# A state-space layer between two gated feed-forward blocks: prologue and first half step in a written-out order

## The chip, the cores and the metric

The kernel runs on one core of a Trainium2 chip. The time is that of the whole program on the device, in microseconds (us), as the median of several runs. Profiles show one execution; its span leaves out a little of the time at the start and end.

## The reference

Input x is [2, 2048, 256] in float32. Three residual parts follow each other:

```python
x = x + 0.5 * ffn(layernorm(x), w_gate, w_up, w_down)
x = x + ssm(layernorm(x), in_proj, conv, x_proj, dt_proj, A_log, D, C_proj, out_proj)
x = x + 0.5 * ffn(layernorm(x), w_gate, w_up, w_down)
# ffn: (silu(x @ wg.T) * (x @ wu.T)) @ wd.T, integer weights times 1/127, hidden width 768
# ssm: x_in, z = split(x @ in_proj.T), width 512 each
#      xc = causal convolution of x_in, 4 taps;  dt, B = split(xc @ x_proj.T)
#      delta = clip(softplus(dt @ dt_proj.T + dt_b), 0.001, 0.1);  a = exp(delta * A)
#      h[t] = a[t] * h[t-1] + (a[t] - 1) / A * B[t];  y = h @ C_proj.T + xc * D
#      out = (y * silu(z)) @ out_proj.T
```

## The kernel before

The 2048 rows of each sequence go in four tiles of 512. The program is a chain of half steps h = -1 to 8 that alternate between the two sequences. In half step h, part **A** is the first feed-forward of one sequence's tile, **B** the state-space layer of the other sequence's tile, **C** the second feed-forward of the tile whose B was one half step earlier. `Bnext` is the layer norm ahead of the next B. Half step -1 has only A, half step 0 has B and A, the last has only C.

Every engine has its program written out, and semaphores tie them. No scheduler moves anything. On TensorE a table gives the order of steps: `gate0` to `gate5` and `up0` to `up5` (a 128 x 512 chunk of the hidden width), `down00` to `down11` (a quarter of the product back to tokens), `ix` and `iz` (chunks of the input projection for x and z), `xp0` and `xp1` (dt and B), `cp0` to `cp3` (the product with C), `out00` to `out11`, and `turn0`, `turn1` (normalized rows turned on TensorE). Products go through four PSUM banks `q` in turn; a bank is free again when the one operation that reads it (ScalarE or VectorE) has run, and the function `plan` counts which one that is. Each float32 operand is taken apart in a high and a low half of 16 bits: ScalarE writes the high one (`xh`, `hh`, `xch`), VectorE or GpSimd the low one (`xl`, `hl`, `xcl`).

The prologue stands ahead of and in half step -1. Weights arrive as 32-bit integers or floats, ScalarE casts them (L487), TensorE turns 128 x 128 blocks into a bank (a "fill", L1257), ScalarE copies the bank to the weight tile (L503 to L526). VectorE reduces the integer weights to their largest size (L1091, L1114), counts those over 256, and the count becomes a flag on which TensorE and VectorE branch (`further_parts`, L1311; here it is zero and the branch is taken past). VectorE computes scales: `hidden_scales` (L936 to L942), `row_scales` (L947 to L953), `conv_bound` and `conv_scale` (L1006 to L1028, with one product on TensorE between them, L1451), `x_proj_scale` (L1040 to L1044), and the constants of A by a series on single columns (`decay_rate`, `decay_series`, `decay_finish`, L959 to L984). In the old order these last three stand in the first half step between the softplus input (L842) and delta (L847).

A fill group is issued as a whole (`early`, `up`, `down`, `in`, `delta`, `late`), and half step 0 uses the same function `half(g)` as all later ones on each engine. On VectorE: `stats` L742, `variance` L750 to L760, `normalize` L773, `norm_lo` L782, `hidden` L803, `residual` L814, the convolution taps L828, `halo` L836, `series` L860, `scan` L885, `skip_y` L899. On ScalarE: `norm_hi` L532, `gate` L550, `hidden_high` L558, `conv_begin` L566, `conv_in` L574, `input_in` L615. On GpSimd: `root` L407, the cast of w_down L413, `hidden_low` L421, `conv_low` L428, `gate_y` L436.

## Time and profile before

| | |
|---|---|
| median of 3 runs | 540.81 us (538.62 to 544.32) |
| the profiled execution | 548.71 us, span 546.8 us |
| TensorE busy | 507.3 us (93%) |
| VectorE busy | 416.7 us (76%) |
| ScalarE busy | 281.1 us (51%) |
| GpSimd busy | 227.0 us (42%) |
| mean granted clock of TensorE | 0.968 |

Times of a profile are counted from the span's start. The granted clock is a share of 2.4 GHz. In the rows, PE is TensorE, DVE VectorE, ACT ScalarE, POOL GpSimd; buffer numbers are left out of names, so `xpre` is the loaded rows of either sequence. An arrow in brackets names what ended the idle time ahead of an instruction.

### The profile page before, as it was taken

Reading aid. Unit: us, or ns where it says so; the run is one execution under the profiler, and the core shown is the slowest. Engines: PE = TensorE matmul, PEld = TensorE weight load, DVE = VectorE, ACT = ScalarE, POOL = GpSimd, SP = SyncE. Lnnn points to the kernel's source line nnn. Section 1 sums busy time; section 2 is a strip of 40 time slices with the busy share of each in tenths; the row PEclk is TensorE's granted clock in tenths of the full one; section 3 lists DMA queues with packets and bytes.
Section 4 is the critical chain, followed back from the end, with each engine's and each line's share of the span. In section 5 each row is a group of like instructions: output and inputs, shape, how many; then the busy total and the mean of one; then the engine's idle time right before and its main releaser. Section 6 shows DMA issues by size and latency. Waiting matters only on the chain.

```text
span 546.8 us, 7716 instructions
## 1 busy us (share of the span) xinstructions
PE 507.3 (93%) x2657; PEld 296.1 (54%) x2657; DVE 416.7 (76%) x865; ACT 281.1 (51%) x472; POOL 227.0 (42%) x192
## 2 busy tenths in 40 slices
PE   4869877999999999999999999999999999998696
PEld 4346423844566465745485456646484557545444
DVE  5786678699678977798769977897869876887332
ACT  5473655076624774187606672377508761674032
POOL 2230053428271637246451828154633736073213
PEclk9887997999999999999999999999999999999869
DMA  8401000000220020101120032003020021000001
GB/s 290 119 0 41 2 0 0 2 2 0 41 80 1 2 41 32 47 1 22 30 69 0 2 41 78 1 2 40 20 59 2 10 33 40 1 1 20 19 2 40
DMA packets 27240, 16.84 MB, mean 31 GB/s; under 512 B 15264, under 2 KB 26528, under 8 KB 27184
## 3 DMA queue, kind: packets, MB, share of 16 engines
q1 hardware_dynamic: 26368, 15.26, 11.1%
q10 hardware_dynamic: 816, 0.79, 0.5%
q8 instruction: 40, 0.66, 0.5%
q14 instruction: 16, 0.13, 0.1%
HBM read 8.71 MB, written 4.19 MB: 24 GB/s over the span
## 4 chain that ended last, share of the span: by engine, by line
PE 73%; DVE 12%; DMA 5%; ACT 3%; issue 3%; SPq 2%; POOL 2%; POOLq 0%; DVEq 0%; ACTq 0%
PE q L1346 49%; PE dp L1346 19%; DMA xt<-xs 4%; DVE xn L773 3%; PE tp L1257 3%; SPq L379 2%; DVE xs L790 2%; DVE h L803 1%; DMA hh<-in_L_ffn_w_gate_dram 1%; POOL xcl L428 1%; PE q L1257 1%; ACT xc L566 0%; DVE rmx L947 0%; DVE ser L860 0%; DVE x L814 0%
## 5 line engine op out<-in xcount | busy, mean ns | idle before, releaser
L421 POOL TENSOR_TENSOR hl<-h,hh 128x512 f16<-128x512 f32 x96 | 121.1, 1274 | 107.2 <-ACT hh L558 106.9
L803 DVE SCALAR_TENSOR_TENSOR h<-sg,hsm,q 128x512 f32<-128x512 f32 x96 | 70.7, 742 | 39.3 <-PE q L1346 26.2
L828 DVE SCALAR_TENSOR_TENSOR xc<-xi,cw,xc 128x512 f32<-128x512 f32 x96 | 84.1, 890 | 3.2 <-ACT xi L574 2.6
L532 ACT ACTIVATE xh<-tp 128x512 f16<-128x512 f32 x36 | 19.5, 595 | 113.8 <-PE tp L1257 113.8
L550 ACT ACTIVATE sg<-q 128x512 f32<-128x512 f32 x96 | 56.6, 591 | 40.8 <-PE q L1346 40.8
L558 ACT ACTIVATE hh<-h 128x512 f16<-128x512 f32 x96 | 60.3, 629 | 27.4 <-DVE h L803 27.1
L428 POOL TENSOR_TENSOR xcl<-xc,xch 128x512 f16<-128x512 f32 x32 | 41.1, 1296 | 50.4 <-ACT xch L581 50.4
L1346 PE MATMUL dp<-wo,yu 128*128 128x256 f32 x256 | 60.2, 388 | 1.5 <-POOL yu L436 1.5
L1346 PE MATMUL dp<-wd,hh 128*128 128x256 bf16 x384 | 53.9, 277 | 0.9 <-ACT hh L558 0.9
L1346 PE MATMUL dp<-wd,hl 128*128 128x256 bf16 x384 | 53.7, 277 | 0.8 <-POOL hl L421 0.8
L1346 PEld LDWEIGHTS dp<-wo,yu 128*128 128x128 f32 x256 | 48.4, 195 | 9.5 <-POOL yu L436 2.7
L1346 PEld LDWEIGHTS dp<-wd,hh 128*128 128x128 f16 x384 | 38.0, 99 | 13.2 <-issue 5.5
L1346 PE MATMUL q<-xh,wu 128*128 128x512 f16 x120 | 37.9, 399 | 5.9 <-ACT bm L615 4.3
L436 POOL TENSOR_TENSOR yu<-yu,sz 128x512 f32<-128x512 f32 x32 | 39.6, 1273 | 8.6 <-DVE yu L899 8.6
L1346 PEld LDWEIGHTS dp<-wd,hl 128*128 128x128 f16 x384 | 38.2, 99 | 6.0 <-issue 1.1
L566 ACT ACTIVATE xc<-q,cb,rw 128x512 f32<-128x512 f32 x32 | 25.0, 780 | 31.3 <-PE q L1346 31.3
L1346 PE MATMUL q<-xh,wg 128*128 128x512 f16 x120 | 37.9, 399 | 2.6 <-DVE xl L782 2.0
L1346 PE MATMUL q<-xh,wih 128*128 128x512 f16 x128 | 38.3, 379 | 1.4 <-ACT xh L532 1.2
L1346 PE MATMUL q<-xt,wg 128*128 128x512 f16 x144 | 37.0, 379 | 2.4 <-DMA xt<-xs 2.4
L1346 PE MATMUL q<-xh,wil 128*128 128x512 f16 x128 | 38.1, 379 | 0.0
L1346 PE MATMUL q<-xl,wih 128*128 128x512 f16 x128 | 38.1, 379 | 0.0
L1346 PE MATMUL q<-xl,wg 128*128 128x512 f16 x120 | 37.7, 396 | 0.0
(182 smaller groups left out, 851.0 us busy)
## 6 DMA issues: line engine op xcount, KB each, us to landing
xpre<-in_L_attn_x_dram SPq DMA_DIRECT2D x8, 512.0 KB, 4.5
out_dram<-x SPq DMA_DIRECT2D x16, 256.0 KB, 2.1
xc<-in_L_attn_in_proj_w_dram SPq DMA_DIRECT2D x1, 1024.0 KB, 11.1
hl<-in_L_ffn_w_up_dram ACTq DMA_DIRECT2D x3, 256.0 KB, 6.5
hh<-in_L_ffn_w_gate_dram SPq DMA_DIRECT2D x3, 256.0 KB, 7.1
hh<-in_L_ffn_w_down_dram SPq DMA_DIRECT2D x1, 768.0 KB, 8.5
yu<-n_L_attn_out_proj_w_dram SPq DMA_DIRECT2D x1, 512.0 KB, 4.0
yu<-in_L_attn_x_proj_w_dram SPq DMA_DIRECT2D x1, 256.0 KB, 11.4
```

The lines of the kernel that those rows point to most:

```text
L421: pool.tensor_tensor(HL[g.f][:, c, :], H[:, j, :], HH[g.f][:, c, :], ALU.subtract)\
L428: pool.tensor_tensor(XCL[:, m, :], XC[g.b][:, m, :], XCH[:, m, :], ALU.subtract)\
L436: pool.tensor_tensor(YU[g.b][:, m, :], YU[g.b][:, m, :], SZ[g.b][:, m, :], ALU.mult)\
L532: act.activation(XH[g.f][:, kc, :], tp[kc][:, :], ACT.Copy, scale=XS).then_inc(t_hi[kc], 1)
L550: act.activation(SG[:, (first + c) % 2, :], q[bank][:, :], ACT.Silu, scale=QUANT / XS)\
L558: act.activation(HH[g.f][:, c, :], H[:, (first + c) % 3, :], ACT.Copy).then_inc(hh_ready, 1)
L566: act.activation(XC[g.b][:, m, :], q[bank][:, :], ACT.Identity, bias=CB[:, m:m + 1], scale=RW3[:, m:m + 1]).then_inc(xc_begun, 1)
L773: ins = dve.tensor_scalar(XN[:, b, :], src[:, b, :], MN[k][:, b:b + 1], RS[k][:, b:b + 1], ALU.subtract, ALU.mult)
L803: dve.scalar_tensor_tensor(out=H[:, first % 3, :], in0=SG[:, first % 2, :], scalar=HSM[:, c:c + 1], in1=q[bank][:, :], op0=ALU.mult, op1=A ...
L828: dve.scalar_tensor_tensor(out=XC[s][:, m, :], in0=XI[s][:, m, k:k + TILE], scalar=CW[:, m, k:k + 1], in1=XC[s][:, m, :], op0=ALU.mult, op ...
L1257: return pe.transpose(dst, src, IDN[:, :] if ident is None else ident)
L1346: ins = pe.matmul(out, w, a, start=(at == 0), stop=(at == len(terms) - 1))
```

## The change

The orders of the prologue and of half step 0 are written out one step at a time on TensorE (a table `FIRST`), ScalarE, VectorE and GpSimd. Fill groups become single fills, so that they stand between chunks of the products. Half steps 1 to 6 keep the function `half`; half steps 7 and 8 are written out too, in the order that they had. No operation is added or removed and no tile changes; the DMA queues keep their order.

```diff
+FIRST = (("fill", "g0", -1), ("fill", "u0", -1), ("fill", "g1", -1), ("fill", "u1", -1), ("count0", "", -1),
+         ("fill", "g2", -1), ("fill", "u2", -1), ("turn0", "A", -1), ("turn1", "A", -1), ("flag0", "", -1),
+         ("more0", "", -1), ("gate0", "A", -1), ("gate1", "A", -1), ("up0", "A", -1), ("gate2", "A", -1),
...
 def tensor_order(h):
-
-
-
-    if h == -1:
...
-    return [(what, part, h) for what, part in ORDER
-            if has("A" if part == "Bnext" else part, h) and (what, part, h) not in done]
...
-    for what, part, h in (step for at in range(-1, LAST + 1) for step in tensor_order(at)):
+    middle = [step for h in range(1, LAST - 1) for step in tensor_order(h)]
+    for what, part, h in (*FIRST, *middle, *FINAL):
...
+            last = "w_dve" if part[:-1] in ("i", "x", "t") else "w_act"
+            count[last] += 1
+            reader[take("ring", part, h)] = (last, count[last])
...
-            hidden_low(Half(-1), "A")
-            root(Half(-1), "Bnext")
-            half(Half(0))
-            for h in range(1, LAST + 1):
+            before, start, late, last = Half(-1), Half(0), Half(LAST - 1), Half(LAST)
+            pool.wait_ge(negh_ready, 1)
+            root(before, "A")
+            root(start, "A")
+            hidden_low(before, "A", (0,))
+            cast_down()
+            hidden_low(before, "A", (1, 2, 3, 4, 5))
+            root(before, "Bnext")
+            conv_low(start, (0, 1, 2, 3))
+            hidden_low(start, "A", (0, 1, 2, 3, 4, 5))
+            gate_y(start, (0, 1, 2, 3))
+            root(start, "Bnext")
...
+            cast("g", 0)
+            cast("u", 0)
+            fill("g0")
+            cast("g", 1)
+            cast("u", 1)
+            fill("u0")
+            cast("g", 2)
+            fill("g1")
+            fill("u1")
+            cast("u", 2)
+            fill("g2")
+            norm_hi(before, "A", (0,))
+            fill("u2")
+            norm_hi(before, "A", (1,))
...
+            norm_hi(start, "A", (0,))
+            scale_row(0)
+            scale_row(1)
+            gate(before, "A", (4,))
+            scale_row(2)
+            norm_hi(start, "A", (1,))
+            hidden_high(before, "A", (2,))
+            scale_row(3)
+            scale_row(4)
+            gate(before, "A", (5,))
+            fill("d0")
+            fill("d1")
+            scale_row(5)
+            scale_row(6)
+            fill("d2")
+            scale_row(7)
+            fill("i0")
+            copy_rank()
+            hidden_high(before, "A", (3,))
+            fill("i2")
+            hidden_high(before, "A", (4, 5))
+            fill("i1")
+            scale_x(0)
+            scale_x(1)
+            fill("i3")
...
-            first, second = Half(-1), Half(0)
-            stats(first, "A", range(NB))
-            variance(first, "A")
-            for j in range(HC // 2):
-                if j == 1:
-                    normalize(first, "A")
-                for nat, load, rows in ((NGI, ld_g, WMX[:, 0:HC]), (NUI, ld_u, WMX[:, HC:2 * HC])):
-                    dve.wait_ge(load[j], 16)
-                    ins = dve.tensor_reduce(rows[:, 2 * j:2 * j + 2], nat[:, 2 * j:2 * j + 2, :], AX.X, ALU.max,
...
+            weight_rows("g", 0)
+            weight_rows("u", 0)
+            weight_rows("g", 1)
+            weight_rows("u", 1)
+            stats(before, "A", (0, 1, 2, 3))
+            weight_rows("g", 2)
+            variance(before, "A")
+            weight_rows("u", 2)
+            stats(start, "A", (0,))
+            over(0)
+            stats(start, "A", (1,))
+            normalize(before, "A", (0, 1, 2, 3))
+            stats(start, "A", (2, 3))
+            hidden_scales()
+            weight_flag(0)
+            norm_lo(before, "A", (0, 1))
+            flags[0] = flag_value(0)
+            variance(start, "A")
+            further_parts(0)
+            weight_rows("d", 0)
+            normalize(start, "A", (0, 1))
+            hidden(before, "A", (0,))
+            normalize(start, "A", (2, 3))
+            hidden(before, "A", (1,))
...
+            variance(before, "Bnext")
+            hidden(start, "A", (0,))
+            normalize(before, "Bnext", (0, 1, 2, 3))
+            decay_rate()
+            x_proj_low(0)
+            norm_lo(before, "Bnext", (0, 1))
+            decay_series()
+            hidden(start, "A", (1,))
+            conv(start, 0, (2, 1, 0))
+            conv(start, 1, (2, 1, 0))
+            conv(start, 2, (2,))
+            x_proj_low(1)
+            conv(start, 2, (1, 0))
+            conv(start, 3, (2, 1, 0))
+            hidden(start, "A", (2,))
+            decay_finish()
+            delta_in(start)
+            stats(Half(1), "A", (0, 1))
+            hidden(start, "A", (3,))
+            delta(start)
+            series(start, (0, 1, 2, 3))
+            decay_out(start)
+            input_out(start)
+            scan(start)
+            halo(start)
+            hidden(start, "A", (4, 5))
+            skip_y(start, (0, 1, 2))
+            residual(start, "A", 0)
+            skip_y(start, (3,))
+            stats(start, "Bnext", (0, 1))
+            residual(start, "A", 1)
+            stats(start, "Bnext", (2, 3))
+            variance(start, "Bnext")
...
                 if B:
-                    if g.h == 0:
-                        decay_rate()
-                        decay_series()
-                        decay_finish()
                     delta(g)
...
+            for step in FIRST:
+                do(*step)
+            for h in range(1, LAST - 1):
+                for step in tensor_order(h):
+                    do(*step)
+            for step in FINAL:
+                do(*step)
```

VectorE, start of the program, before. `wmx` holds the largest integer weights (`hh` and `hl` are the buffers in which gate and up weights arrive), `over` the count behind the flag, `xn` the normalized rows of the first sequence:

```order
L742 BN_STATS st_A<-xpre 128x6 x4
...
L760 TENSOR_TENSOR ve_A<-vo_A,vi_A 128x4
L1091 TENSOR_REDUCE wmx<-hh 128x2
L1091 TENSOR_REDUCE wmx<-hl 128x2
L773 TENSOR_SCALAR xn<-xpre,mn_A,rs_A 128x256 x4
L1091 TENSOR_REDUCE wmx<-hh 128x2
...
L919 TENSOR_SCALAR over<-wmx 128x12
...
L782 SCALAR_TENSOR_TENSOR xl<-tp,xh 128x512 x2
```

and now, where `hsc` belongs to the hidden scales:

```order
L1050 TENSOR_REDUCE wmx<-hh 128x2
L1050 TENSOR_REDUCE wmx<-hl 128x2
...
L869 BN_STATS st_A<-xpre 128x6 x4
L1050 TENSOR_REDUCE wmx<-hh 128x2
...
L887 TENSOR_TENSOR ve_A<-vo_A,vi_A 128x4
L1050 TENSOR_REDUCE wmx<-hl 128x2
L869 BN_STATS st_A<-xpre 128x6
L1063 TENSOR_SCALAR over<-wmx 128x12
...
L900 TENSOR_SCALAR xn<-xpre,mn_A,rs_A 128x256 x4
L869 BN_STATS st_A<-xpre 128x6 x2
L1080 TENSOR_TENSOR hsc<-wmx 128x6
...
L909 SCALAR_TENSOR_TENSOR xl<-tp,xh 128x512 x2
```

Two reductions stood between the variance and the normalized rows; now four reductions stand ahead of the statistics, and statistics of the second sequence, the count and the hidden scales stand among normalized rows and low half.

ScalarE, end of half step -1, before. `hh` is the high half of the hidden product, `xc` here the rows of the input projection's weights that are scaled, `wd` and `wih` the weights of down and of the input projection, `da` the copy of the rank weights:

```order
L558 ACTIVATE hh<-h 128x512
...
L695 ACTIVATE xc<-xc,rsc 128x256 x4
L558 ACTIVATE hh<-h 128x512
L508 ACTIVATE wd<-q,hsi 128x256
L509 ACTIVATE wd<-q,hsi 128x256
...
L498 ACTIVATE da<-tp 16x128
L512 ACTIVATE wih<-q 128x512 x4
```

and now:

```order
L558 ACTIVATE xc<-xc,rsc 128x256 x2
L529 ACTIVATE wd<-q,hsi 128x256
L530 ACTIVATE wd<-q,hsi 128x256
L558 ACTIVATE xc<-xc,rsc 128x256
L533 ACTIVATE wih<-q 128x512
L545 ACTIVATE da<-tp 16x128
L590 ACTIVATE hh<-h 128x512
L533 ACTIVATE wih<-q 128x512
L590 ACTIVATE hh<-h 128x512 x2
L533 ACTIVATE wih<-q 128x512
```

The last hidden copies moved from ahead of the weights of down to between the weights of the input projection.

VectorE, half step 0, before. `xc` is now the convolution's output (12 taps), `sp` the softplus input, `er` to `ia` the constants of A, `dl` delta, `bb` the scan's input, `hs` its output:

```order
L828 SCALAR_TENSOR_TENSOR xc<-xi,cw,xc 128x512 x12
L842 TENSOR_SCALAR sp<-q,dtb 128x512
L959 TENSOR_SCALAR er<-al 128x1
...
L971 TENSOR_SCALAR ey<-ey,er 128x1 x6
...
L984 TENSOR_TENSOR ia<-ia,xri 128x1
L847 TENSOR_SCALAR dl<-sp 128x512
...
L877 SCALAR_TENSOR_TENSOR bb<-sp,bm 128x512
L803 SCALAR_TENSOR_TENSOR h<-sg,hsm,q 128x512 x2
L836 COPY xi<-xi 128x4x3
L885 SCALAR_TENSOR_TENSOR hs<-sp,carry,bb 128x512
L803 SCALAR_TENSOR_TENSOR h<-sg,hsm,q 128x512 x2
```

and now:

```order
L955 SCALAR_TENSOR_TENSOR xc<-xi,cw,xc 128x512 x7
L1145 TENSOR_TENSOR wxl<-q,wxh 128x512
L955 SCALAR_TENSOR_TENSOR xc<-xi,cw,xc 128x512 x5
L930 SCALAR_TENSOR_TENSOR h<-sg,hsm,q 128x512
L1119 TENSOR_SCALAR e<-ek 128x1
...
L1128 TENSOR_TENSOR ia<-ia,xri 128x1
L969 TENSOR_SCALAR sp<-q,dtb 128x512
L869 BN_STATS st_A<-xpre 128x6 x2
L930 SCALAR_TENSOR_TENSOR h<-sg,hsm,q 128x512
L974 TENSOR_SCALAR dl<-sp 128x512
...
L1004 SCALAR_TENSOR_TENSOR bb<-sp,bm 128x512
L1012 SCALAR_TENSOR_TENSOR hs<-sp,carry,bb 128x512
```

The constants left the place between `sp` and `dl`, and the hidden products `h` and the copy `xi` no longer stand ahead of `hs`.

## Rows read from the trace of the kernel before

**Rows 1.** The page, part 1: busy time and share of the span by engine.

```profile
PE 507.3 (93%) x2657; PEld 296.1 (54%) x2657; DVE 416.7 (76%) x865; ACT 281.1 (51%) x472; POOL 227.0 (42%) x192
```

**Rows 2.** Windows, TensorE: stretch, its us, busy us (instructions), granted clock, DMA share, GB/s.

```profile
0.00:109.39 109.39, 84.89 (x418) 0.91 0.18 57
109.39:546.80 437.41, 422.40 (x2241) 0.98 0.11 24
16.76:19.60 2.84, 2.84 (x8) 0.50 0.84 267
28.00:36.00 8.00, 3.71 (x22) 1.00 0.00 0
37.00:47.12 10.12, 9.25 (x39) 0.50 0.01 2
85.00:91.69 6.69, 6.00 (x15) 0.51 0.00 0
```

**Rows 3.** Waits of TensorE up to 109 us: who ended them, in total, times, longest.

```profile
PE q L1346 <- ACT bm L615: 4.3, 1, 4.3
...
PE tp L1451 <- DVE bb L1013: 2.2, 1, 2.2
```

**Rows 4.** Timeline of VectorE at the start: start us, busy us, instruction, [idle before].

```profile
6.06 1.41 DVE L742 BATCH_NORM_STATS2 st_A<-xpre 128x6 f32<-128x256 f32 x4 [5.13 <-DMA xpre<-in_L_attn_x_dram]
...
8.28 0.68 DVE L1091 TENSOR_REDUCE wmx<-hh 128x2 f32<-128x512 int32 x1
...
9.58 1.38 DVE L773 TENSOR_SCALAR xn<-xpre,mn_A,rs_A 128x256 f32<-128x256 f32 x4
...
14.58 1.27 DVE L782 SCALAR_TENSOR_TENSOR xl<-tp,xh 128x512 f16<-128x512 f32 x2
```

**Rows 5.** Timeline of TensorE: the first gate chunk and the first down product.

```profile
16.29 0.81 PE L1346 MATMUL q<-xh,wg 128*128 128x512 f16 x2 [2.02 <-DVE xl L782]
...
42.36 1.46 PE L1346 MATMUL dp<-wd,hh 128*128 128x256 bf16 x6
```

**Rows 6.** Timeline of ScalarE: second load of gate weights; last hidden copy, first product.

```profile
8.94 0.63 ACT L487 ACTIVATE sz<-hh 128x512 f32<-128x512 int32 x1 [0.69 <-DMA hh<-in_L_ffn_w_gate_dram]
...
35.02 0.62 ACT L558 ACTIVATE hh<-h 128x512 f16<-128x512 f32 x1
```

**Rows 7.** Tile xpre up to 30 us: issue of the second load, and time to landing.

```profile
L355 SPq DMA_DIRECT2D xpre<-in_L_attn_x_dram x1: 474/474/474, 4.1 to 4.1; - x1
...
DMA to landing us min/median/max: 5.3/7.2/9.1
```

**Rows 8.** Timeline of VectorE from 22 to 91 us.

```profile
22.57 3.06 DVE L773 TENSOR_SCALAR xn<-xpre,mn_A,rs_A 128x256 f32<-128x256 f32 x4 [0.19 <-POOL rs_A L407]
...
51.57 0.67 DVE L1001 TENSOR_TENSOR wxl<-q,wxh 128x512 f16<-128x512 f32 x1
...
63.03 10.64 DVE L828 SCALAR_TENSOR_TENSOR xc<-xi,cw,xc 128x512 f32<-128x512 f32 x12 [2.65 <-ACT xi L574]
76.29 0.75 DVE L842 TENSOR_SCALAR sp<-q,dtb 128x512 f32<-128x512 f32 x1 [2.61 <-PE q L1346]
...
81.56 0.43 DVE L847 TENSOR_SCALAR dl<-sp 128x512 f32<-128x512 f32 x1
...
86.51 0.74 DVE L803 SCALAR_TENSOR_TENSOR h<-sg,hsm,q 128x512 f32<-128x512 f32 x1
...
89.09 2.25 DVE L885 TENSOR_TENSOR_SCAN hs<-sp,carry,bb 128x512 f32<-128x512 f32 x1
```

**Rows 9.** The page, part 5: GpSimd's low halves and the convolution taps, whole run.

```profile
L421 POOL TENSOR_TENSOR hl<-h,hh 128x512 f16<-128x512 f32 x96 | 121.1, 1274 | 107.2 <-ACT hh L558 106.9
...
L828 DVE SCALAR_TENSOR_TENSOR xc<-xi,cw,xc 128x512 f32<-128x512 f32 x96 | 84.1, 890 | 3.2 <-ACT xi L574 2.6
```

**Rows 10.** Timeline of TensorE: C products of the first half step; first product of the next.

```profile
92.93 3.60 PE L1346 MATMUL q<-hs,wc 128*128 128x512 f32 x8
...
109.39 0.59 PE L1346 MATMUL q<-xh,wih 128*128 128x512 f16 x2
```

More of the change, by code:

```diff
@@ L1134, in _ @@
-            variance(first, "Bnext")
-            x_proj_low(1)
-            normalize(first, "Bnext")
-            hidden(second, "A", (0, 1))
-            norm_lo(first, "Bnext")
-            x_proj_unscale()
             def half(g):
@@ L1245, in half @@
                     stats(ahead, "C", (0, 1))
-            half(Half(0))
-            for h in range(1, LAST + 1):
-                half(Half(h))
+            before, start, late, last = Half(-1), Half(0), Half(LAST - 1), Half(LAST)
+            weight_rows("g", 0)
[6 more added lines that the diff above has]
+            weight_rows("u", 2)
@@ new lines, in _ @@
+            normalize(start, "Bnext", (2, 3))
+            stats(Half(1), "C", (0, 1))
+            for h in range(1, LAST - 1):
+                half(Half(h))
+            norm_lo(Half(6), "Bnext", (0, 1))
+            residual(Half(6), "B", 1)
+            stats(late, "C", (2, 3))
+            variance(late, "C")
+            normalize(late, "C", (0, 1))
+            conv(late, 0, (2,))
+            normalize(late, "C", (2,))
+            conv(late, 0, (1,))
+            normalize(late, "C", (3,))
@@ new lines, in _ @@
+            delta(late)
+            series(late, (0, 1, 2, 3))
+            decay_out(late)
+            input_out(late)
+            halo(late)
+            scan(late)
+            residual(late, "C", 0)
+            skip_y(late, (0, 1, 2, 3))
+            residual(late, "C", 1)
+            residual(late, "B", 0)
+            carry(late)
+            stats(last, "C", (0, 1))
+            residual(late, "B", 1)
+            stats(last, "C", (2, 3))
+            variance(last, "C")
+            normalize(last, "C", (0, 1, 2, 3))
@@ L1437, in half @@
-            def half(g):
-                run(tensor_order(g.h), g)
-            steps, first = tensor_order(-1), Half(-1)
-            products = steps.index(("gate0", "A", -1))
-            rows = steps.index(("fill", "in", -1))
-            delta_rows, tokens = steps.index(("fill", "delta", -1)), steps.index(("down00", "A", -1))
-            run(steps[:products], first)
-            count_over(0)
-            flag = flag_value(0)
-            further_parts(flag, [p for p in PARTS if p[0] != "d"])
@@ L1448, in _ @@
-            run(steps[products:rows], first)
-            pe.wait_ge(xm_ready, 1)
-            pe.matmul(tp[1][:, 0:P], XMB, IDN[:, :], start=True, stop=True).then_inc(xm_full, 1)
-            run(steps[rows:delta_rows], first)
-            count_over(1)
-            run(steps[delta_rows:tokens], first)
-            flag_down = flag_value(1)
-            further_parts(flag_down, [p for p in PARTS if p[0] == "d"])
-            run(steps[tokens:], first)
-            half(Half(0))
-            for h in range(1, LAST + 1):
-                half(Half(h))
+            flags = {}
```

461 lines of the change are left out of this document (277 added, 184 removed), and 25 rows, old and new, of tables (FINAL, FIRST).

## The prediction

> **What bounds the kernel now.** I read the page first: TensorE is busy 507.3 of 546.8 us, VectorE 416.7 [rows 1]. Then the windows [rows 2], cut where the first half step ends on TensorE (109.39 us): up to there TensorE is busy 84.89 us, after it 422.40 of 437.41 us. So the later half steps are at TensorE's floor, and 24.5 of the 39.5 idle us lie in the stretch that the change rewrites. The granted clock is at its half level (0.50, 1.2 of 2.4 GHz) there three times: 2.84, 10.12 and 6.69 us [rows 2]; busy time at half rate is half lost, (2.84 + 9.25 + 6.00) / 2 = 9.0 us. The list of waits [rows 3] says what ends TensorE's idle time: apart from the loads at the start 4.3 us for the state input that ScalarE scales and 2.2 for the bound are the longest. The last view is the timeline, for the moment at which each stage starts.
>
> The order of instructions after the first half step is the same in both programs on every engine, and TensorE hardly waits there. So what the first 109.39 us lose or gain arrives at the end one for one. The work is the same too; only its order, and the engine instruction that stands ahead of which, change. I therefore walk the new order from marker to marker with durations of the old trace. "Start to start" spacing is used, which is a little below the durations printed: 0.60 us for a weight reduction, 0.65 for a 128x512 VectorE operation, 0.55 for a ScalarE one, 0.86 for a gate or up chunk (two matmul pairs of 0.43), 1.30 for an input projection chunk, 0.48 for a weight turned through a bank, 1.31 for a quarter of the down product.
>
> **The first gate chunk: 3.4 us later.** Before, VectorE takes the statistics of the first rows at 6.06 and writes the normalized rows from 9.58; the first gate chunk starts at 16.29 [rows 4, 5]. Now four weight reductions stand ahead of the statistics. The second pair of loads lands at 8.94 [rows 6], so they end at 10.1; statistics 1.3 (11.4); a reduction (12.0); the variance 0.8 (12.8); a reduction (13.4); the root on GpSimd 1.0, hidden. Then statistics of the second sequence, whose load lands 9.1 us after its issue at 4.1, at 13.2 [rows 7]; two blocks and the count cost 0.9 (14.3); normalizing 1.3 (15.6); two more blocks 0.7; the hidden scales, now ahead of the flag, 1.4 (17.7); the flag 0.25; two low halves 1.3 (19.2). TensorE's branch on the flag waits for the second low half, as before, and came 0.5 us behind it (14.58 + 1.27 to 16.29). The first gate comes at 19.7, +3.4 us. The half-rate spell behind that wait I keep at its 2.84 us: it is idle again for some 3 us ahead of it.
>
> **From there to the variance ahead of the input projection: 5.0 us won.** Before it ends at 52.9 (the seven small operations of 0.8 us, a subtraction from 51.57 in front, [rows 8]). The gates of the first sequence now run in the order gate, gate, up, gate, up, with the turns of the next rows split in two. The four normalizing operations took 3.06 us while GpSimd's low halves ran, against 1.38 where it did not [rows 4, 8]; now they stand at 22.7 and 24.7, ahead of GpSimd's first low half at 25.3, so 1.3. The row scales end at 30.0. From there ScalarE has no gap: eight row scalings of 0.4, two gates, two norm halves, six copies for down, three of four input weights, the rank copy, and the four hidden copies, 10.5 us in all, and the last hidden copy ends at 40.5; before it was put ahead of the weights and ended at 35.6 [rows 6]. GpSimd's last three low halves, 1.2 each [rows 9], end at 42.6. So the down product, which began at 42.36 at half rate [rows 5], begins at 40.6 but cannot end its first quarter before 42.7; three more at full rate give 46.7. Residual, statistics and variance follow to 49.9, with three input-weight subtractions between them on VectorE. That is with the full clock. TensorE's idle pieces between 33 and 41 us are shorter than before (2.4 us; 4.3 between 28 and 36 us before), but not gone, and a 2.0 us gap was enough to bring the half level at 16.76 [rows 2, 5]. I take the half level here too, at 1.4 us of delay for the variance (the down quarters end 2.3 later, 0.9 of it under the subtractions). End of the variance 51.3: 1.6 us ahead of before. Bounds of this term: 0 and 4.6 (half level through all of the down product).
>
> **To the start of the convolution: 2.0 us won.** Before, four chunks and five weight fills precede the turn and the convolution starts at 63.03 [rows 8]. Now three chunks precede it; one weight subtraction, one hidden product and two fills are put off. From the variance: hidden 0.65, normalize 1.35 with the root, rate constants 1.3, a subtraction 0.65, two low halves 1.3 (they wait for ScalarE), the series of constants 1.65, hidden 0.65: 8.1 us, start at 59.4, with ScalarE's shifted copy 0.5 us ahead of it.
>
> **To delta: 2.7 us won.** Before, 12 taps of 0.88, a wait of 2.61 for the projection, then 4.6 us of one-column constants alone between the softplus input (76.29) and delta (81.56) [rows 8]. Now the taps with one subtraction take 11.3, a hidden product and the last constants (2.3) fill the wait, and behind the input come only 0.75 of statistics and 0.65 of hidden under ScalarE's exponential and logarithm (1.6). From 59.4: 70.7, 73.0, 73.7, delta at 75.3.
>
> **To the end of the scan: 2.4 us won.** Series and outputs keep their 4.9 us; two hidden products and the halo copy, 2.6 us from 86.51 to 89.09, no longer stand ahead of the scan [rows 8]. Delta to scan end was 9.7, now 7.3: 82.6 instead of 91.3. That these are put behind it costs cover: the last hidden products are now on the way to the down product. C products start right at the scan's end (before at 92.93, behind chunks at half rate), three of them take 2.6; hidden 4 and 5 end 2.2 after the scan, the last low half 2.5 later, so the down product waits 0.8 us.
>
> **To the end of the half step: 0.3 us won.** From 92.93 to 109.39 TensorE is without a gap [rows 10]: four C products, down, out, a turn, 16.5 us. The same work plus 0.8 for the low half, and 0.5 because the turn waits for a normalization that now straddles a residual: 17.8 from the scan's end, against 18.1. End at 100.4.
>
> Sum: -3.4 + 5.0 + 2.0 + 2.7 + 2.4 + 0.3 = **9.0 us won**. The profiled execution took 548.7 us, so 539.7; the three runs have a median of 540.81, 1.4% below it, and I take the same difference there: **531.8 us**. The shares saved hang on idle time, not on the level of the run.
>
> **A page's rule that speaks against it.** In this trace TensorE goes through the four banks with a reader behind each product from 109.39 on, at a mean granted clock of 0.98 [rows 2]; short waits did not pull it down there. The Trainium skill, "TensorE: Matmul & The Clock Gate", section "A second HAM failure mode: psum-queue depth-cycling", says that going through PSUM banks with small idle pieces between groups makes the clock go back and forth and loses throughput although few matmuls look slow. By that rule the finer interleaving would be slower, not faster; the trace of before does not show it in its steady part, but 37 to 47 us looks like it. What it would cost is the third case below, from rows.
>
> **The cases.** Less than 1% (5.4 us) can't be told from no change here.
> - *As walked*, 62%: 9.0 us, from 5.8 (the 4.6 bound) to 11.8 (no half level at 37 us, +1.4, and a warm start, +1.4). 529 to 535.
> - *All half levels go and the early loss is smaller*, 10%: two of the six weight reductions may slip under the wait for the second load. 10.4 + 1.4 + 1.5: 527.5.
> - *The ring eats it*, 20%: each bank is freed by one named operation, and VectorE and ScalarE run in the written order. Two places are tight: iz1 waits for the subtraction that stands behind seven taps, and the down product for hidden copies at the end of a 10.5 us ScalarE queue. Taps that GpSimd slows (890 ns in the mean [rows 9]) by another 0.2 us each cost 2.4; each ScalarE operation 0.1 late costs 2. With the half level bound of 3.2 more, 9.0 becomes 1.4: 534 to 541, same.
> - *Slower*, 8%: TensorE stays at 1.2 GHz from about 30 to 63 us of the new order. The walk has some 25 us of full-rate work there and 6 us of slack, so 19 us more: 540.8 - 10.4 + 19 = 549. It decides from where half-rate work exceeds 16 us beyond the slack, that is when the low spells there last over 30 us; before they last 10.12 [rows 2]. Against it: fewer and shorter gaps than before. A spell that reaches 25 us gives only "same".
>
> That the order doesn't take hold is excluded, since order and waits are fixed at build; that it hides is too, as TensorE waits under 4% after 109.39.
>
> **Numbers.** Predicted 531.8; range 525 to 539 (the second case, less 2.5 of spread between runs, to the middle of the third). Faster by over 1%: 0.62 x 0.95 + 0.10 + a little of the third, 0.70. Same 0.22, slower 0.08.
>
> **What would show it.** First gate chunk at 19.7 with the idle time before it ended by the second low half; last hidden copy of the first product at 40.5 and its low half at 42.6; convolution from 59.4; nothing but statistics and a hidden product between softplus input and delta; scan ending at 82.6; first product of the next half step at 100.4; no half level near 85 us; the rest as long as before (437.4). Wrong if the first gate comes at 17 or at 22, if the clock row is at 5 for most of 30 to 60 us, or if TensorE's idle time ahead of the C products stays over 3 us.

## The result, and the profile after

The changed kernel took **537.6 us** in the median of 20 runs (534.59 to 541.34), the kernel before, beside it, 544.45 us (20 runs, 538.48 to 548.79): ratio 0.9888, 95% interval 0.9867 to 0.991, so 6.1 us won by the ratio and 6.9 by the two medians. The time of the changed kernel lies in the range forecast. The gain is less than the 9.0 us of the sum, and the 531.8 us are 5.8 too low.

The profiled execution took 536.74 us (span 534.9), the one of before 548.71. The page, part 1, answers to [rows 1]: TensorE is busy 8.0 us less with the same 2657 matmuls, so it ran longer at full rate.

```profile
PE 499.3 (93%) x2657; PEld 291.1 (54%) x2657; DVE 415.5 (78%) x865; ACT 280.0 (52%) x472; POOL 226.8 (42%) x192
```

Windows of TensorE, after (stretch, its us, busy us and instructions, granted clock, DMA share, GB/s), cut at the first product of the next half step, 99.25 us. They answer to [rows 2].

```profile
0.00:99.25 99.25, 79.12 (x418) 0.95 0.20 63
99.25:534.90 435.65, 420.14 (x2241) 0.99 0.10 24
13.90:24.44 10.54, 7.98 (x28) 0.52 0.51 141
28.00:36.00 8.00, 7.37 (x42) 1.00 0.00 0
30.00:50.00 20.00, 17.00 (x112) 1.00 0.02 5
80.00:95.00 15.00, 13.25 (x77) 1.00 0.01 2
```

The first half step is 10.1 us shorter, the rest 1.8. One stretch at the half level is left in front (0.52 from 13.90 to 24.44 us), and it is longer than the 2.84 us of before, which I had kept. The two others are gone in this execution: 1.00 from 28 to 36, from 30 to 50 and from 80 to 95 us.

The waits of TensorE up to 99.25 us, after (who ended them: total us, times, longest), answer to [rows 3]:

```profile
PE q L1566 <- DVE xl L909: 2.6, 1, 2.6
PE dp L1520 <- DVE over L1063: 2.2, 1, 2.2
PE dp L1566 <- POOL hl L427: 1.9, 2, 1.0
PE q L1471 <- ACT xc L558: 1.1, 1, 1.1
```

The 4.3 and 2.2 us of [rows 3] are gone. TensorE now waits 2.2 us for the count (`over`) and 2.6 us for the low half, both ahead of the first gate chunk; behind it no wait is longer than 1.1 us.

Timeline of TensorE, after (start us, busy us, instruction, [idle before, who ended it]), against [rows 5, 10]:

```profile
19.37 1.01 PE L1566 MATMUL q<-xh,wg 128*128 128x512 f16 x2 [2.56 <-DVE xl L909]
...
40.98 0.83 PE L1566 MATMUL dp<-wd,hh 128*128 128x256 bf16 x6
...
43.33 0.28 PE L1566 MATMUL dp<-wd,hl 128*128 128x256 bf16 x1 [0.97 <-POOL hl L427]
...
81.30 2.84 PE L1566 MATMUL q<-hs,wc 128*128 128x512 f32 x6 [0.78 <-DVE hs L1012]
...
99.25 0.60 PE L1566 MATMUL q<-xh,wih 128*128 128x512 f16 x2
```

The first gate chunk starts at 19.37 behind the low half of the normalized rows, as walked. The down product starts early but its last hidden low half holds it up at 43.33, also as walked; then it runs at full rate. The C products start at the scan's end.

Timeline of VectorE, after, against [rows 8]:

```profile
49.79 0.16 DVE L887 TENSOR_TENSOR ve_Bnext<-vo_Bnext,vi_Bnext 128x4 f32<-128x4 f32 x1
...
57.53 5.22 DVE L955 SCALAR_TENSOR_TENSOR xc<-xi,cw,xc 128x512 f32<-128x512 f32 x7
...
72.22 0.75 DVE L969 TENSOR_SCALAR sp<-q,dtb 128x512 f32<-128x512 f32 x1
72.88 0.74 DVE L869 BATCH_NORM_STATS2 st_A<-xpre 128x6 f32<-128x256 f32 x2
73.54 0.73 DVE L930 SCALAR_TENSOR_TENSOR h<-sg,hsm,q 128x512 f32<-128x512 f32 x1
74.57 0.43 DVE L974 TENSOR_SCALAR dl<-sp 128x512 f32<-128x512 f32 x1 [0.30 <-ACT sp L633]
...
79.96 1.28 DVE L1012 TENSOR_TENSOR_SCAN hs<-sp,carry,bb 128x512 f32<-128x512 f32 x1
```

Between the softplus input (72.22) and delta (74.57) stand only statistics and one hidden product, against 5.3 us before. The scan starts 5.4 us behind delta, not 7.5.

### The profile page after: what moved, and what is told of

It is laid out like the page before. It is cut to its first block, busy times and chain, and to the rows that moved or that the text cites. A ratio compares the mean times of both kernels' runs of the same rounds, so it can differ in the third digit from the quotient of the medians.

```text
span 534.9 us, 7722 instructions
## 1 busy us (share of the span) xinstructions
PE 499.3 (93%) x2657; PEld 291.1 (54%) x2657; DVE 415.5 (78%) x865; ACT 280.0 (52%) x472; POOL 226.8 (42%) x192
## 4 chain that ended last, share of the span: by engine, by line
PE 70%; DVE 13%; DMA 5%; issue 4%; ACT 4%; POOL 2%; SPq 2%; POOLq 0%; ACTq 0%; DVEq 0%
PE q L1566 47%; PE dp L1566 19%; DMA xt<-xs 3%; PE tp L1471 3%; DVE xn L900 3%; DVE h L930 2%; DVE xs L917 1%; SPq L388 1%; DVE xc L955 1%; DMA hh<-in_L_ffn_w_gate_dram 1%; POOL hl L427 1%; DVE x L941 1%; ACT xc L558 1%; DVE hs L1012 1%; ACT sg L582 0%
## 5 line engine op out<-in xcount | busy, mean ns | idle before, releaser
L564 ACT ACTIVATE xh<-tp 128x512 f16<-128x512 f32 x36 | 19.7, 598 | 116.5 <-PE tp L1471 116.5
L1566 PE MATMUL dp<-wo,yu 128*128 128x256 f32 x256 | 58.6, 381 | 1.5 <-POOL yu L442 1.5
L1566 PE MATMUL dp<-wd,hh 128*128 128x256 bf16 x384 | 52.7, 273 | 1.0 <-ACT hh L590 0.9
L1566 PEld LDWEIGHTS dp<-wo,yu 128*128 128x128 f32 x256 | 47.2, 190 | 9.1 <-POOL yu L442 2.7
L1566 PE MATMUL q<-xh,wu 128*128 128x512 f16 x120 | 36.7, 388 | 0.7 <-ACT sg L582 0.7
## 6 DMA issues: line engine op xcount, KB each, us to landing
xc<-in_L_attn_in_proj_w_dram SPq DMA_DIRECT2D x1, 1024.0 KB, 10.9
```

The source lines that it names most:

```text
L564: act.activation(XH[g.f][:, kc, :], tp[kc][:, :], ACT.Copy, scale=XS).then_inc(t_hi[kc], 1)
L1566: ins = pe.matmul(out, w, a, start=(at == 0), stop=(at == len(terms) - 1))
```

## The experiments

**Does the gain hang on the level that an execution happens to have?** The two kernels were run again unchanged, before four times (before_r1 to r4) and after three times (after_r1 to r3), each with a profile; before_r1 and after_r1 were also timed.

> The kernel before, unchanged, profiled a second time. Theory 1 (the forecast's size failed because its sum was made against one profiled execution in which TensorE's half clock level lasted longer than usual: 20.5 us in the first 109 us and 13.7 us in the last 35): this profile has a span shorter than 546.8 us by 2 to 6 us, with less half-level time, and the same busy order otherwise. Theory 2 (the profile was typical, and the later half steps eat part of the gain in most executions): span 546 to 548 and half-level time of about 34 us again. Ratio to the kernel before 1.000 either way, which shows how finely this measurement can tell.

> The changed kernel, profiled a second time. Theory 1: first product of the next half step again at 99 to 101 us, the rest within 1.5 us of 435.7, so a span of 534 to 538 us; ratio 0.987 to 0.991. Theory 2: the rest after that product is 438 us or more, span 538 to 541.

> The kernel before, unchanged, a third profile: how its own executions differ. If chance in the half-level spells makes the size of the gain: the first product of the next half step comes somewhere between 103 and 109 us, earlier where the half level in the first 110 us is shorter, and a marker under 107 us appears in one of the two further profiles. If the marker is fixed (108 to 109.5 in every execution), the missing 2 to 3 us of the forecast are lost behind the marker.

> The kernel before, a fourth profile; expectations as for the third.

> The kernel before, a fifth profile. Its marker was 109.4, 108.2, 103.3 and 104.6 so far, with a half-level spell of 10.2, 10.2, 3.4 and 3.4 us from about 37 us on. If the spell's length sets it: 103 to 105 with a short one, 108 to 110 with a long one, nothing between but for the spell near 85 us.

> The changed kernel, unchanged, a third profile. If chance in the half level moves it too: marker between 98 and 101.5, later where a spell falls on the stretch from 31 to 48 us. If not: 99.2 again.

> The changed kernel, a fourth profile. So far the marker was 99.25, 99.22 and 98.82. If the new order takes the chance out of the clock: 98.5 to 99.6 again.

Measured: before_r1 545.31 us, ratio 0.999 (0.9959 to 1.002); after_r1 537.78 us, 0.9888 (0.9846 to 0.993). The starts of the stages in every profile (us of the span):

| | gate | variance | convolution | delta | scan | C products | next half step | span |
|---|---|---|---|---|---|---|---|---|
| before, first | 16.29 | 52.85 | 63.03 | 81.56 | 89.09 | 92.93 | 109.39 | 546.8 |
| before_r1 | 16.40 | 53.10 | 63.29 | 81.80 | 89.34 | 91.65 | 108.21 | 544.0 |
| before_r2 | 15.68 | 49.62 | 59.81 | 78.33 | 84.68 | 86.80 | 103.25 | 537.0 |
| before_r3 | 15.35 | 49.24 | 59.42 | 77.94 | 84.29 | 88.09 | 104.55 | 542.0 |
| before_r4 | 16.19 | 52.77 | 62.95 | 81.47 | 89.00 | 92.86 | 109.32 | 546.8 |
| walked for after | 19.7 | 51.3 | 59.4 | 75.3 | | | 100.4 | |
| after, first | 19.37 | 49.79 | 57.53 | 74.57 | 79.96 | 81.30 | 99.25 | 534.9 |
| after_r1 | 19.17 | 48.73 | 56.48 | 74.53 | 79.92 | 81.26 | 99.22 | 534.3 |
| after_r2 | 19.78 | 49.34 | 57.09 | 74.13 | 79.52 | 80.86 | 98.82 | 535.2 |
| after_r3 | 18.95 | 48.50 | 56.24 | 73.28 | 78.67 | 80.01 | 97.96 | 534.8 |

One program, before, reaches its second half step anywhere from 103.25 to 109.39 us, and behind that point it takes from 433.7 to 437.5 us more. Windows of TensorE in before_r2:

```profile
30.00:50.00 20.00, 15.50 (x109) 0.91 0.04 11
80.00:95.00 15.00, 12.53 (x72) 1.00 0.01 1
```

and in before_r1:

```profile
30.00:50.00 20.00, 15.52 (x85) 0.74 0.01 2
80.00:95.00 15.00, 10.74 (x36) 0.89 0.00 0
```

The granted clock from 30 to 50 us is 0.91 in one and 0.74 in the other, in the same stretch of the same program. The timelines of TensorE show what hangs on it. Before_r2:

```profile
41.50 0.83 PE L1346 MATMUL dp<-wd,hh 128*128 128x256 bf16 x6 [0.68 <-issue]
...
46.09 0.82 PE L1346 MATMUL dp<-wd,hl 128*128 128x256 bf16 x6
```

and before_r1:

```profile
42.46 1.46 PE L1346 MATMUL dp<-wd,hh 128*128 128x256 bf16 x6
...
46.28 1.49 PE L1346 MATMUL dp<-wd,hl 128*128 128x256 bf16 x6
```

Six products of down take 0.83 us in one and 1.46 in the other; the variance ends 3.5 us later. Near 85 us it is the same: 1.00 in before_r2 against 0.89 in before_r1 (0.77 in the first profile and before_r4), and the scan starts 6.4 us behind delta in r2 and r3, 7.5 in the others. Before_r3 has 0.89 there too, but its half level sets in at 83.4 us only, behind the product that the two hidden operations ahead of the scan read. After_r1 to r3 have 0.91, 1.00 and 0.91 from 30 to 50 us and 1.00 from 80 to 95 in all. So the change does not always keep the half level out of 30 to 50 us: two of its four profiles have as much there as before_r2. In front, from 12 to 30 us, its clock is lower: 0.72, 0.81, 0.91 and 0.81, against 0.91, 0.91, 0.91, 1.00 and 0.91 in the five of before. So the first profile of before, on which the sum was made, was one of the two worst of five. The mean of its five second half steps is 106.9 us, of the four after 98.8.

**Is it the half level, and does it matter that TensorE idles?** Products of the identity with itself ("fillers"), into a bank that nobody reads at that moment, were put into TensorE's gaps.

```
+ def keep_busy(n, bank=dp[1]):
+     for _ in range(n):
+         pe.matmul(bank[:, 0:P], IDN[:, :], IDN[:, :], start=True, stop=True)
  before_warm: 32 at the start, 15 ahead of the flag, 12 ahead of up5 A -1,
               16 ahead of the bound, 34 ahead of up3 A 0
  after_warm:  32 at the start, 17 ahead of count0, 20 ahead of flag0, 8 ahead of fill i1
```

> The kernel before with extra matmuls of the identity into an unused bank wherever TensorE idles in the first 86 us: 32 ahead of the first weights, 15 ahead of the first flag, 12 ahead of up5, 16 ahead of the bound, 34 ahead of up3 of half step 0. They fill idle time and change no order. Theory 1: the half level disappears from the first 110 us; the first product of the next half step comes 5 to 9 us earlier than in the old profile (109.4), and the timed ratio is 0.985 to 0.993, since a typical execution of the kernel before loses some 4 to 6 us to it. Theory 2: half-level time in the kernel before is small in most executions, so the ratio is 0.995 to 1.002.

> The changed kernel with the same filler matmuls: 32 ahead of the first weights, 17 ahead of the count, 20 ahead of the first flag, 8 ahead of the third input fill. Theory 1 (the new order gains by waits and by fewer half-level spells; its own remaining spell at 14 to 24 us costs about 2.5 us): ratio to the kernel before 0.982 to 0.986, that is 2 to 4 us under the changed kernel; against the kernel before with fillers it keeps only the wait part, 3 to 5 us. Theory 2 (clock does not matter to the size): ratio as of the changed kernel, 0.989.

Measured: before_warm 546.57 us, ratio 1.0036 (1.001 to 1.0062), after_warm 538.70, 0.9891 (0.9852 to 0.9929). As a test of gain they failed, since one such product in float32 is two passes of 0.12 us, twice what I had counted: the first gate chunk was held up to 18.77 and 24.12 us. The clock from 12 us to the next half step was 1.00 in both profiles, and the runs lay closer together, 545.63 to 548.47 (12 runs) and 538.17 to 539.36 (6), than the same kernels without fillers beside them (5.1 us for 12 runs, 4.6 for 6). After_warm's first gate came 4.8 us late, its next half step at 101.37, 2.6 us behind the mean of after, and its median 0.9 us above that of after_r1. Smaller numbers of fillers:

```
  before_fill: 16, 6, 7, 5 and 16 at those places, and 16 into tp[0] ahead of turn0 C LAST
  after_fill:  16; 6, 7 and 3 at those places; 16 into tp[0] ahead of turn0 C LAST
  after_tail:  only the last 16
```

> The kernel before with fillers that are half as long as in before_warm (a filler is two passes of 0.12 us, which had been counted as one), so that they end inside the idle time: 16 ahead of the first weights, 6 ahead of the first flag, 5 ahead of up5, 7 ahead of the bound, 16 ahead of up3 of half step 0; and 16 in the 4.5 us ahead of the last layer norm's turn. Theory 1 (a typical execution of the kernel before loses several us to the half level, and the amount is chance): the times draw together (lowest to highest under 4 us, against 7.6 to 10 for the kernel before) and the ratio is 0.982 to 0.993. Theory 2 (the half level is not what the spread is from): ratio 0.997 to 1.002, spread 7 us or more.

> The changed kernel with such fillers: 16 ahead of the first weights, 6 ahead of the count, 7 ahead of the first flag, 3 ahead of the third input fill, 16 ahead of the last turn. Theory 1: 3 to 5 us below the changed kernel (ratio to the kernel before 0.979 to 0.983), spread under 3 us; the distance to before_fill is what the new order wins by waits alone, 4 to 7 us, less than the 9.0 forecast. Theory 2: ratio 0.988 as without fillers, distance to before_fill 9 us.

> The changed kernel with fillers only ahead of the last layer norm's turn, 16 of them in a wait of 4.9 us, none in the prologue. If the half level behind that wait (6.8 to 10 us in every profile so far) costs what its rows say, about half of its busy time: 2 to 3 us under the changed kernel, ratio 0.983 to 0.985, and the rest behind the marker 433 to 434 us instead of 435 to 436.3. If after_fill won in the prologue alone: ratio 0.988, rest 435.

Measured: after_fill **532.72 us**, 0.9759 (0.9727 to 0.9792), 5 us below the changed kernel and with old_fill (below) the fastest; after_tail 535.66, 0.9871 (0.9824 to 0.9918); before_fill 543.6, 0.997 (0.9939 to 1.0001). Windows of TensorE, after_fill:

```profile
12.00:30.00 18.00, 14.38 (x85) 1.00 0.42 122
96.58:530.02 433.44, 420.84 (x2273) 1.00 0.10 25
490.00:530.00 40.00, 31.20 (x173) 1.00 0.08 27
```

and after_tail:

```profile
12.00:30.00 18.00, 13.39 (x58) 0.72 0.40 120
490.00:530.00 40.00, 33.00 (x179) 1.00 0.06 21
```

The granted clock is 1.00 in all of these stretches of after_fill; its second half step starts at 96.58, 2.2 ahead of the mean of after. After_tail keeps 0.72 in front, as the changed kernel does, and has 1.00 in the last turn's stretch (0.91, 0.96, 0.91 and 0.87 from 490 to 530 in the four profiles of after). In the profiles the part behind the next half step's start takes 433.4 us in after_tail and in after_fill, 435.0 to 436.8 in the four of after: about 2.5 us of the 5 at the end, 2.2 in front. The timed runs can't confirm the share of the end: after_tail's ratio, 0.9871, is not apart from the changed kernel's 0.9888. Nor did the last filler always work: before_fill and old_fill have the same one and 0.96 and 0.91 from 490 to 530.

Before_fill missed its expectation. The ratio is that of "the half level is not what the spread is from", the spread of 5.0 us fits neither case, and it lies 10.9 us above after_fill, not 4 to 7. Its timeline of TensorE:

```profile
37.60 0.19 PE L1309 MATMUL dp<-over,one 128*1 128x2 f32 x2
39.48 2.04 PE L1301 MATMUL q<-dl,da 16*128 16x512 f32 x2 [1.69 <-DVE wil L993]
41.45 1.46 PE L1353 MATMUL dp<-wd,hh 128*128 128x256 bf16 x6
```

No filler stood between 37.8 and 39.5 us, where TensorE waits 1.69 us for the low half of an input weight; the products behind it run at half rate (1.46). Its second half step starts at 105.51, only 1.4 ahead of the mean of before. That this gap is why the half level stayed is not shown: after_fill waits 1.72 us ahead of its first gate chunk, at 19.15, and keeps 1.00 there.

**What is the late first gate worth?** The old order of the first rows in the new kernel:

```
  VectorE: stats(before), variance, two weight_rows, normalize, four weight_rows,
           over(0), stats(start, 0), flag, low halves, stats(start, 1 to 3), hidden_scales
  TensorE: turn0 and turn1 ahead of fill g2, u2, count0, flag0
```

> The changed kernel with the old order at the start of VectorE, TensorE and ScalarE: statistics and variance of the first rows ahead of the weight reductions, turns ahead of the last two fills, count behind them, the flag ahead of the hidden scales; all else new. If the first term of the forecast (the new start costs 3.4 us, and this reaches the end) is right: first gate chunk at 16.0 to 16.6, first product of the next half step 1.5 to 3 us earlier than 99.2, ratio 0.983 to 0.986. If the start is hidden behind the loads and ScalarE's queue: gate early, but the marker unchanged within 0.7 us and ratio 0.987 to 0.990.

> Two edits that won apart, together: the changed kernel with the old order at its start and with fillers (16 ahead of the first weights, 1 ahead of the count, 5 ahead of the flag, 4 ahead of gate5 of the first product, 3 ahead of the third input fill, 16 ahead of the last turn). If they add up: first gate at 15.8, marker at 94.5 to 96, 1 to 2 us under after_fill (532.7), ratio 0.972 to 0.976. If ScalarE's queue from 30 us on is what counts: marker as in after_fill, 96.6, ratio 0.976.

Measured: after_oldstart 537.52 us, 0.9847 (0.9815 to 0.988); old_fill (the same with fillers) 532.85, 0.9766 (0.9739 to 0.9793). Timeline of TensorE, after_oldstart:

```profile
16.62 0.62 PE L1564 MATMUL q<-xh,wg 128*128 128x512 f16 x2 [2.02 <-DVE xl L908]
...
29.87 0.60 PE L1564 MATMUL q<-xh,wg 128*128 128x512 f16 x2 [1.39 <-DVE h L929]
...
39.16 0.83 PE L1564 MATMUL dp<-wd,hh 128*128 128x256 bf16 x6
```

The first gate comes 2.75 us earlier, the down product 1.8 and the next half step, at 98.45, 0.8 against the first profile of after, 0.4 against the mean. TensorE waits again at 29.87, for VectorE. By the ratio (0.9847 against 0.9888) the early gate would be worth 2.2 us, by the medians 0.1; the marker's 0.8 lies between the two ranges expected.

The reduction that gives the row scales of the state input, and behind it ScalarE's queue, starts at 24.84 in after_oldstart, 24.33 in after_fill and 23.88 in old_fill, though the gate chunks start up to 3.4 us apart. In these three, VectorE's own work ahead of that reduction sets what follows, and the late gate is nearly free: after_fill and old_fill end 0.1 us apart. In the changed kernel without fillers the reduction starts later, at 25.46 to 27.14. There the first gate chunks run at half rate (1.01 to 1.06 us for two products, later 0.59), and in the first profile VectorE waits for them. Its timeline, after:

```profile
24.69 0.75 DVE L930 SCALAR_TENSOR_TENSOR h<-sg,hsm,q 128x512 f32<-128x512 f32 x1 [1.81 <-PE q L1566]
```

After_oldstart has its variance at 47.97, 1.8 us ahead of the first profile of after, and loses 1.0 of it again ahead of the softplus input, where one product on a single column takes 1.17 us beside GpSimd (the last section has the same in after_r1). Old_fill loses 1.0 in the same place: its next half step, at 97.36, is behind after_fill's. So what the late gate costs alone stays open between 0 and 2 us.

**One term by itself.** The rate constants alone moved in the kernel before, and alone put back in the changed one:

```
before_consts                             after_consts_back
+ decay_rate(); decay_series()            - decay_rate(); decay_series()   (ahead of the taps)
    (behind the unscaling of x_proj)      - decay_finish()   (ahead of delta_in)
+ decay_finish()  (ahead of delta_in)     + all three behind delta_in
- the three behind delta_in
```

> The kernel before with one part of the change alone: the constants of A on VectorE leave the place between softplus input and delta (rate and series ahead of the convolution, the rest ahead of the softplus input, which then waits less). By the forecast's term for this stretch: delta 2.7 us earlier (78.9), scan start at 86.4, first product of the next half step 2 to 4 us earlier than 108.2 to 109.4, ratio 0.992 to 0.996. If TensorE's half-rate chunks and not VectorE set the end of this stretch: delta earlier, marker within 1 us, ratio 0.998 to 1.001.

> The changed kernel with one part undone: the constants of A stand again on VectorE between softplus input and delta. By the forecast (2.7 us of the 9.0 in this stretch, and the half level near 85 us gone because TensorE no longer waits 4.3 us there): softplus input at about 70 to 71, delta at 76.5, marker 1.5 to 4 us later than 99.1, ratio 0.991 to 0.996. If other waits cover it: ratio 0.988 to 0.990.

Measured: before_consts 541.86 us, 0.9925 (0.9893 to 0.9957); after_consts_back 538.54, 0.9902 (0.9873 to 0.9932). Timeline of VectorE, before_consts:

```profile
71.96 0.93 DVE L976 TENSOR_TENSOR na<-ey,e 128x1 f32<-128x1 f32 x1
...
74.54 0.75 DVE L842 TENSOR_SCALAR sp<-q,dtb 128x512 f32<-128x512 f32 x1 [0.45 <-PE q L1346]
76.90 0.43 DVE L847 TENSOR_SCALAR dl<-sp 128x512 f32<-128x512 f32 x1 [1.60 <-ACT sp L599]
```

and after_consts_back:

```profile
69.80 0.75 DVE L969 TENSOR_SCALAR sp<-q,dtb 128x512 f32<-128x512 f32 x1 [1.72 <-PE q L1566]
70.47 0.14 DVE L1103 TENSOR_SCALAR er<-al 128x1 f32<-128x1 f32 x1
...
76.38 0.42 DVE L974 TENSOR_SCALAR dl<-sp 128x512 f32<-128x512 f32 x1
```

Moved alone, they bring delta from 5.3 to 2.36 us behind the softplus input, and about 4 us in time, more than the 2.7 walked for them; the next half step starts at 101.82 in its profile. Put back, delta falls 6.58 us behind the input and the next half step starts at 101.05, 1.8 to 3.1 us late, but the median is only 0.9 us above the changed kernel's. The profiled execution of after_consts_back was the slowest of its 11 runs. The first is clear, the second is inside what these runs tell apart. The term that was walked largest, 5.0 us to the variance, was not run by itself.

## Where the prediction failed, and where it was right

The direction was right, and so was the mechanism in the main: TensorE's two long waits went. The step that failed is the last, where the sum was made against one profiled execution, "The profiled execution took 548.7 us, so 539.7", and carried over to the median of three runs with "I take the same difference there" and "The shares saved hang on idle time, not on the level of the run." Two things are wrong in it.

- *The base.* 540.81 was the median of three runs; 20 runs have 544.45. That is 3.6 us of the miss of 5.8. A kernel whose runs reach from 538 to 549 needs more than three.
- *The level.* The profile was 7.9 us above the median of three and 4.3 above that of 20. It had the long stretches at the half level, and the sum counted their removal as won in every execution. They are not there in every one: the saved shares do hang on the level of the run. The first profile's second half step at 109.39 stands 2.4 us above the mean of five (106.9); 9.0 less 2.4 is 6.6, and 6.1 to 6.9 were timed. That these meet is in part luck, since the profiles themselves show a gain at this marker of 10.1 us in the first pair and of 8.1 in the mean, not of 9.0 and 6.6. Against before_r2, which has the least of the half level, the marker of after_r2 is only 4.4 us ahead. How much of the gain is order alone is not shown: before_r2 still falls to the half level three times ahead of its marker, after_r2 once. Before_warm and after_warm, both at 1.00 there, are 6.7 us apart at the marker and 7.9 in their medians, but their fillers hold them up by different amounts.

The terms, first profile against first profile, beside those of the pair with the least half level, before_r2 against after_r2:

| term | walked | first pair | r2 pair |
|---|---|---|---|
| first gate chunk | -3.4 | -3.1 | -4.1 |
| to the variance | +5.0 | +6.1 | +4.4 |
| convolution | +2.0 | +2.4 | +2.4 |
| delta | +2.7 | +1.5 | +1.5 |
| end of the scan | +2.4 | +3.1 | +1.0 |
| to the next half step | +0.3 | 0.0 | -0.7 |
| sum | +9.0 | +10.1 | +4.4 |

- *First gate chunk.* Right in size (19.37 against 19.7), but little of it reached the next half step: given back, it brings 0.4 to 0.8 us there. A term at the head of a walk is no full loss where another engine's queue is late anyway. The stretch at the half level there, kept at 2.84 us in the walk, took 10.5 in the first profile.
- *To the variance.* The last hidden low half of the first product ended at 43.02 (42.6 walked; row 39.64 of GpSimd in the last section), and down's last product of the first quarter came behind it. The half level that I assumed at 37 us for 1.4 us of delay did not come in the first profile, and 1.1 us were won beyond the forecast. That the one is the reason for the other is not shown: after_r1 and after_r3 have the half level there (six down products in 1.46 us), and their stage is no longer than after_r2's without it, 29.6 us in all three.
- *Convolution.* Met, 2.4 against 2.0; the seven pieces listed for it add to 7.55 us, not to 8.1, and 7.74 were measured.
- *Delta.* Walked 2.7, measured 1.5. One operation on one column, 0.16 us in before, took 1.15 us beside GpSimd, and the logarithm held delta for 0.3 us. In after_r1 a second one was caught, and delta came 1.0 us later still.
- *Scan.* 3.1 against 2.4 in the first pair: C started at the scan's end, as walked, and the scan took 1.28 us, not 2.25. In the r2 pair the scan of before was short too, and the gain is 1.0.
- *The slower case.* It did not come. The changed kernel goes through the four banks in a finer order, and the granted clock from 28 to 63 us was 1.00 in the first profile and in after_r2; in after_r1 and after_r3 it was 0.95, with one fall at 39 us. The rule of the Trainium skill, "TensorE: Matmul & The Clock Gate", section "A second HAM failure mode: psum-queue depth-cycling", would have had it go back and forth there; these traces do not agree.
- *The other cases.* "All half levels go" came true for two of three stretches in the first profile; the one in front stayed and grew. "The ring eats it" fell: its two places cost 0.97 us at 43.33 and nothing visible at the taps (898 ns each, against 890).

**Open.** The profiles show more gain than the timed runs: 8.1 us at the marker and 8.6 in the time of the profiled executions (545.2 mean of five, 536.6 of four), against 6.1 to 6.9. The four profiled executions of after lie 0.6 to 1.6 us below its timed medians. Whether the executions without a profile have a stretch at the half level that these four lack, I cannot show. The five profiled executions of before lie between 538.9 and 548.7 us, so a mean of five may itself be off by the 2 us in question.

## What to carry to other kernels

Before a sum is made against a profile, profile the same kernel several times and see which of its stages differ: what differs by itself, as the half level behind a gap did here, enters the sum with its mean, not with its worst. A serial chain of small operations on one column belongs under the wait ahead of the stage that needs it, and away from GpSimd's work. Idle pieces in TensorE's order that stand ahead of a fall of the granted clock can be worth filling, with real work or with products into an unread bank: after_fill won 5 us so. Keep them short, since too many held up the first gate chunk, and look at several profiles, since before_fill and old_fill still fell.

## What the runs showed of the hardware that was not expected

**VectorE and GpSimd shut each other out, even for a single column.** Timeline of VectorE and GpSimd, after; first VectorE:

```profile
69.82 1.15 DVE L1120 TENSOR_TENSOR na<-ey,e 128x1 f32<-128x1 f32 x1
71.00 0.15 DVE L1121 TENSOR_SCALAR a<-na 128x1 f32<-128x1 f32 x1
...
81.16 1.06 DVE L963 COPY xi<-xi 128x12 f32<-128x12 f32 x1
```

then GpSimd:

```profile
39.64 3.38 POOL L427 TENSOR_TENSOR hl<-h,hh 128x512 f16<-128x512 f32 x3 [4.59 <-ACT hh L590]
...
69.80 1.15 POOL L434 TENSOR_TENSOR xcl<-xc,xch 128x512 f16<-128x512 f32 x1 [1.29 <-ACT xch L615]
70.91 2.29 POOL L427 TENSOR_TENSOR hl<-h,hh 128x512 f16<-128x512 f32 x2
80.20 3.10 POOL L427 TENSOR_TENSOR hl<-h,hh 128x512 f16<-128x512 f32 x2 [7.00 <-ACT hh L590]
83.61 2.27 POOL L427 TENSOR_TENSOR hl<-h,hh 128x512 f16<-128x512 f32 x2 [0.31 <-ACT hh L590]
```

The one-column product that starts at 69.82 ends at 70.97, just behind GpSimd's operation (69.80 to 70.95). With GpSimd idle it takes 0.16, as in the first profile of before:

```profile
80.15 0.16 DVE L976 TENSOR_TENSOR na<-ey,e 128x1 f32<-128x1 f32 x1
```

Chance has a part in it. The last constant, again one column of two inputs, starts 1.10 to 1.11 us behind the start of GpSimd's two low halves in nine profiles of the changed kernel and its variants, about when the first of them ends. In six it takes 0.16 us; in after_r1, after_oldstart and old_fill it lasts as long as the second low half. Timeline of VectorE, after_r1:

```profile
70.97 1.18 DVE L1128 TENSOR_TENSOR ia<-ia,xri 128x1 f32<-128x1 f32 x1
```

GpSimd's two low halves from 80.20 take 3.10 us instead of 2.27, since the scan (79.96 to 81.24, shown above) was there first; and the copy of 12 columns behind it takes 1.06 us.

Timeline of GpSimd in the first profile of before:

```profile
88.00 2.27 POOL L421 TENSOR_TENSOR hl<-h,hh 128x512 f16<-128x512 f32 x2 [9.96 <-ACT hh L558]
```

There the scan of [rows 8] started at 89.09, as the second of these low halves was due, and took 2.25 us instead of 1.28. The Trainium skill, "SBUF — State Buffer", section "SBUF: two separate sides", says that the port pair the two share is locked for a whole instruction by whichever starts first, for VectorE when it reads two inputs from SBUF or runs in a performance mode that uses two ports; the durations of the two-input operations agree. A one-input operation of the same chain (71.00) kept its 0.15 us while GpSimd was busy; the four normalizing ones, one input too but 256 columns, did not: 3.06 us beside GpSimd [rows 8] and 1.38 without [rows 4]. Whether they run in such a mode no run here shows.

**One program, many levels.** The mean granted clock of the profiled executions was 0.968, 0.975, 0.984, 0.977 and 0.968 for before and 0.984, 0.987, 0.990 and 0.980 for after. With the two levels of 1.00 and 0.50 that is 17 to 35 us of the span at the half level for one program and 10 to 22 for the other, and the runs of before reached over 10 us. In after_fill's profile the clock was 1.00 throughout, and its six runs lay within 2.3 us. That the fillers made them lie closer is not shown: six runs of after_oldstart, without fillers, lay within 1.7.
